# Attention block: row maxima carried to q's extra row by four column transfers a half, in place of a transpose, a copy and one transfer

## Chip, cores and metric

The kernel runs on one core of one Trainium2 chip. The metric is device time in microseconds (us) of one execution; the number compared is the median over runs. All times of the kernel before are from three timed runs and one profiled execution.

## What is computed

The input `x` is (16, 512, 32, 32) float32. Each batch entry is group-normalised over 32 groups, read as 1024 tokens of 512 channels, put through attention with 8 heads of size 64, projected with a bias, and added to `x`. Cut to what matters:

```python
xs  = reshape(group_norm(x), (B, T, C))          # B=16, T=1024, C=512
q   = einsum('btc,hcd->bhtd', xs, Wq)            # the same for k and v
att = softmax(einsum('bhtd,bhsd->bhts', q, k) / 8)
out = einsum('bhts,bhsd->bhtd', att, v)          # heads put side by side
y   = x + reshape(out @ Wproj + bproj, x.shape)
```

## The kernel before

There are 16 batch entries of 8 heads, so 128 heads. A head is worked in one *step* of 16 *slots*. In every slot TensorE (PE) issues two matmuls of scores (`scores`, L708 and L709) three blocks ahead, and three matmuls of probabilities times values (L881 to L883): 128x512 outputs each. ScalarE (ACT) takes the exponential of each block of scores twice (L899, to `prob` and, rounded, to `prob_h`), and GpSimd (POOL, L1294, 13 blocks of 16) or VectorE (DVE, L1043) forms the rounding remainder `prob_l`. A buffer ring of two for `prob` and three for `prob_h` and `prob_l` couples the four engines.

The scores are formed transposed (keys in partitions), so the maximum of a query's row can't be subtracted as a bias. It goes in as a 65th row: `q_lm` has 65 rows, rows 0 to 63 for the low part of q and row 64 (`q_lm[D]`) for the negated row maximum, against a row of ones in `k_h1`. A head's maxima are found during the step before it. Sixteen *row blocks* (`row_scores`, L715, one matmul each into one of two PSUM banks `SM`) have the queries in partitions; DVE reduces each to one column of `smax` (`take_max`, L1106). After row blocks 7 and 15 DVE combines eight columns of `smax` into four columns of `nmax` (`combine`, L1111): the maxima of 512 queries, one 128-query tile a column. That is a *half*. Then, for each half, an entry `mt` of the table follows: PE transposes the four columns into a row bank (`turn_rows`, L700), DVE copies the 4x128 result to `mrow` (`take_rows`, L1117), and the sync engine's queue (SP) issues one transfer of `mrow` to 512 elements of row 64 (`max_row`, L546). PE waits for half 0 at the first score block of the next head, which it issues in slot 13 of the step, and for half 1 at the ninth, which it issues in slot 5 of the next step (`mrow_in`, 16 counts each).

What else PE does stands in a table `WORK` written out by hand, one entry for each kind of step: `plain`, `values`, `norm`, `tokens`, `next`, `proj`, `rows`, `end`. For each slot it lists what is done between scores and values (first tuple) and after the values (second tuple): units of q and k (`qk`, `qn`, 12 matmuls each, L663), of values (`v`, 24 half-width matmuls, L675), transposes of tokens (`xt`, L681), of the projection (`proj`, 12, L693), row blocks (`row`) and `mt`. Between two batch entries the steps are two `values`, `norm`, two `plain`, `tokens`, `next` and `proj`; in the last entry `plain`, `rows` and `end` take the place of those that prepare a next one. `turns` in class `Step` gives the row blocks and the `mt` entries the two `SM` banks in turn and tells PE what to wait for (`turn_free`). Other tables say in which slot DVE takes statistics (`STAT_SLOTS`) and normalises (`NORM_SLOTS`), in which slot the softmax sums travel (`DEN_SLOTS`: `den` from `acc`, L572; `INV_SLOTS`: the reciprocal, L1239; `ROWS_SLOTS`: `inv_dram` L577 and `inv_b` L579; `OUT_SLOTS`: POOL's multiplication, L1321), and `LATE` in which slots ACT copies filler results ahead of the exponentials.

Every engine works through its slots in program order, SP too: an entry in SP's list that waits holds up all behind it. SP also issues the copies of q and k to the other half of the partitions (`twice`, L553 and L555), the inputs and the outputs (L588, L592, L620, L624). A `row` 0 needs the first `twice` of its head, row 4 the second.

Of the kernel before, what the change touches and what calls it, by code (L numbers as in the profile page):

```python
# [5 lines left out]
F32 = mybir.dt.float32  # L6
# [21 lines left out]
        ((("qn", 0, 5),), ()),  # L28
        ((), (("mt", 1, 1), ("qn", 0, 2), ("row", 0, 1))),
        ((), ()),  # L30
        ((), (("qn", 0, 1), ("qn", 1, 1), ("row", 0, 1))),
        ((), (("row", 0, 2),)),
        ((), ()),
        ((("row", 0, 1), ("qn", 1, 1)), (("row", 0, 1),)),
        ((("row", 0, 1),), (("qn", 0, 4), ("row", 0, 2))),
        ((), ()),
        ((("mt", 0, 1), ("row", 0, 1)), ()),
        ((), ()),
        ((("row", 0, 2),), ()),
        ((), (("row", 0, 2),)),  # L40
        ((), (("qn", 1, 10),)),
        ((("row", 0, 2),), ()),
# [3 lines left out]
        ((("v", 0, 13),), ()),  # L46
        ((), (("row", 0, 1), ("mt", 1, 1), ("v", 0, 10))),
        ((("row", 0, 2),), (("v", 1, 2),)),
        ((), (("row", 0, 1),)),
        ((), (("v", 0, 1), ("row", 0, 2))),  # L50
        ((("v", 1, 22), ("row", 0, 1)), (("qn", 0, 2),)),
        ((("row", 0, 1),), (("row", 0, 1),)),
        ((), (("qn", 1, 1), ("qn", 0, 4))),
        ((), ()),
        ((("row", 0, 2), ("qn", 1, 2)), (("mt", 0, 1), ("qn", 0, 5), ("qn", 1, 1))),
        ((), (("row", 0, 2),)),
        ((), ()),
        ((), (("row", 0, 2), ("qn", 0, 1))),
        ((), (("qn", 1, 8),)),
        ((), (("row", 0, 1),)),  # L60
# [5 lines left out]
        ((("mt", 1, 1),), (("row", 0, 2),)),  # L66
        ((), (("row", 0, 1),)),
        ((("row", 0, 1),), (("qn", 0, 1),)),
        ((), (("row", 0, 1),)),
        ((), (("row", 0, 2), ("mean", 0, 1), ("qn", 0, 3))),  # L70
        ((("row", 0, 1),), (("row", 0, 1), ("var", 0, 1))),
        ((), (("mt", 0, 1),)),
        ((), (("qn", 0, 1),)),
        ((), (("row", 0, 1),)),
        ((("qn", 1, 2),), (("qn", 0, 1), ("row", 0, 2))),
        ((), (("qn", 1, 1),)),
        ((("qn", 1, 1),), (("row", 0, 1), ("qn", 1, 2))),
        ((("row", 0, 1),), (("qn", 1, 6),)),
# [15 lines left out]
        ((), ()),
        ((("xt", 4, 4),), ()),
        ((), (("row", 0, 2),)),
# [3 lines left out]
        ((("xt", 5, 4),), ()),  # L100
        ((), (("xt", 6, 4),)),
        ((("mt", 1, 1),), (("qk", 0, 12),)),
        ((), (("xt", 7, 4),)),
        ((), ()),
# [9 lines left out]
        ((), (("row", 0, 2),)),  # L114
        ((), ()),
    ),
    "proj": (
        ((), ()),
        ((("mt", 1, 1),), (("row", 0, 2),)),
        ((), (("row", 0, 2),)),  # L120
        ((), (("row", 0, 2), ("proj", 0, 12))),
        ((), (("row", 0, 2), ("proj", 1, 12))),
        ((), (("row", 0, 1),)),
        ((("mt", 0, 1),), (("proj", 2, 12),)),
        ((), (("proj", 3, 12), ("row", 0, 2))),
        ((), ()),
        ((("proj", 4, 12),), (("row", 0, 1),)),
        ((), (("row", 0, 1), ("proj", 5, 12))),
        ((("row", 0, 1),), (("proj", 6, 12),)),
        ((("row", 0, 1),), (("proj", 7, 12),)),  # L130
        ((), (("qn", 0, 12), ("qn", 1, 10))),
        ((("row", 0, 1), ("qn", 1, 2)), ()),
# [4 lines left out]
        ((), (("mt", 1, 1), ("row", 0, 2))),  # L137
# [7 lines left out]
        ((), (("mt", 0, 1), ("row", 0, 1))),  # L145
# [9 lines left out]
        ((), (("mt", 1, 1),)),  # L155
# [19 lines left out]
STAT_SLOTS = ((1, 4, 4, 5), (3, 3, 5, 7))  # L175

MEAN_SLOTS = (6, 7)

NORM_SLOTS = ((13, 15, 15, 15), (11, 12, 14, 15))

DEN_SLOTS = (9, 1)

INV_SLOTS = (10, 2)
# [3 lines left out]
OUT_SLOTS = (13, 5)  # L187
# [3 lines left out]
EARLY_ROWS, EARLY_OUT = (12, 3), (13, 4)  # L191
# [3 lines left out]
CAST_SLOTS = (0, 1, 2, 3, 4, 6, 7, 9)  # L195
SPLIT_SLOTS = tuple(slot + 1 for slot in CAST_SLOTS)

LATE = {"plain": (0, 1, 2, 3, 4, 6, 7, 8, 9, 13, 14), "tokens": (1, 2, 3, 7, 8, 11, 14), "next": (0, 1, 3, 6, 7, 8, 9, 10, 11, 12, 14, 15), "proj": (4, 5, 7, 8, 12, 14), "values": (2, 3, 5, 6, 8, 9, 10, 13, 14), "norm": (0, 1, 4, 7, 8, 9, 10, 12, 15)}


def step_kind(h, has_next, proj):
    if proj:
        return "proj"
    if h in (1, 2):
# [1186 lines left out]
```

## Time and profile before

| | us |
|---|---|
| median of 3 runs (4452.08 to 4463.26) | 4452.45 |
| profiled execution, its own time | 4452.18 |
| span in the profile, first to last instruction | 4450.4 |
| PE busy with matmuls | 4410.9 (99% of the span) |
| ACT busy | 2952.8 (66%) |
| POOL busy | 2857.7 (64%) |
| DVE busy | 2580.5 (58%) |

How to read it: matmuls are pipelined, so a matmul's duration (396 ns for a 128x512 one) covers more than its turn in the array; the distance from one start to the next tells what it costs. "Busy" says little of whether PE waited a few tenths of a microsecond. The view of waits names what ended each idle stretch, the chain of waits follows the last instruction back to what released it, and the timeline has single instructions in order of time. SPq rows are transfers being issued by the sync engine; the time to landing is counted from the issue.

### The profile page before, as it was taken

To read this page: it belongs to the slowest core of one execution; us is meant where nothing else is said; L and a number is where in the kernel's file an instruction comes from. 1 tells how busy PE (TensorE), PEld (TensorE's weight loads), DVE (VectorE), ACT (ScalarE), POOL (GpSimd) and SP (SyncE) were. 2 spreads that over 40 slices of the span, in tenths; PEclk is the share of its full clock that TensorE was granted. 3 is DMA by queue.
4 is the path that set the end of the run, shared out by engine and by line. 5 is a ranking of instruction groups with operands and counts; after the bars stand their busy time and mean duration, and the time that the engine had idled before them with its cause. 6 is when DMAs were issued, how large, how long until landed. Compare 5 with 4: busy or idle time off the path is not lost.

```text
span 4450.4 us, 61770 instructions
## 1 busy us (share of the span) xinstructions
PE 4410.9 (99%) x20864; PEld 3611.6 (81%) x20864; DVE 2580.5 (58%) x5063; ACT 2952.8 (66%) x5644; POOL 2857.7 (64%) x2227
## 2 busy tenths in 40 slices
PE   8999999999999999999999999999999999999999
PEld 7888888888888888888888888887888888888886
DVE  6655646556465565655656556565664656646454
ACT  5766757667576675756757567575775757757575
POOL 5666666666666566665666656666666666567566
PEclk9999999999999999999999999999999999999999
DMA  3111121211111112111121111211112111121201
GB/s 78 38 53 49 37 61 34 57 45 38 59 37 58 43 35 64 36 60 39 33 70 35 56 39 34 68 38 55 38 33 68 39 57 36 36 66 38 59 25 56
DMA packets 156825, 211.42 MB, mean 48 GB/s; under 512 B 56544, under 2 KB 57568, under 8 KB 156512
## 3 DMA queue, kind: packets, MB, share of 16 engines
q1 hardware_dynamic: 156512, 207.47, 16.5%
q8 instruction: 169, 2.77, 0.3%
q14 instruction: 144, 1.18, 0.1%
HBM read 105.12 MB, written 34.08 MB: 31 GB/s over the span
## 4 chain that ended last, share of the span: by engine, by line
PE 94%; DVE 2%; POOL 1%; ACT 1%; DMA 1%; issue 0%; SPq 0%; POOLq 0%; ACTq 0%; DVEq 0%
PE bank L663 16%; PE bank L715 10%; PE bank L881 10%; PE bank L882 10%; PE bank L883 10%; PE bank L709 10%; PE bank L708 10%; PE bank L675 8%; PE bank L693 8%; PE bank L681 1%; POOL prob_l L1294 1%; PE bank L700 1%; DVE smax L1106 1%; DVE xs L1073 0%; ACT prob L899 0%
## 5 line engine op out<-in xcount | busy, mean ns | idle before, releaser
L1294 POOL TENSOR_TENSOR prob_l<-prob,prob_h 128x512 fp32r<-128x512 f32 x1660 | 2140.5, 1297 | 1437.9 <-ACT prob_h L899 1418.2
L1106 DVE TENSOR_REDUCE smax<-bank 128x1 f32<-128x512 f32 x2048 | 1347.5, 682 | 868.2 <-PE bank L715 864.1
L899 ACT ACTIVATE prob<-bank 128x512 f32<-128x512 f32 x2048 | 1232.2, 602 | 575.3 <-PE bank L709 413.1
L899 ACT ACTIVATE prob_h<-bank 128x512 fp32r<-128x512 f32 x2048 | 1227.2, 599 | 461.9 <-PE bank L883 393.0
L881 PE MATMUL bank<-prob_h,vh 128*128 128x512 f32 x2048 | 822.2, 401 | 7.8 <-ACT acc L1018 4.2
L708 PE MATMUL bank<-q_hh,k_hl 128*128 128x512 f32 x2048 | 813.1, 397 | 0.0
L709 PE MATMUL bank<-q_lm,k_h 65*128 65x512 f32 x2048 | 811.4, 396 | 0.0
L882 PE MATMUL bank<-prob_h,vl 128*128 128x512 f32 x2048 | 806.3, 394 | 0.0
L883 PE MATMUL bank<-prob_l,vh 128*128 128x512 f32 x2048 | 805.8, 393 | 0.0
L715 PE MATMUL bank<-k_hl,q_hh 128*128 128x512 f32 x2048 | 716.4, 402 | 6.2 <-DVE smax L1106 6.0
L881 PEld LDWEIGHTS bank<-prob_h,vh 128*128 128x128 f32 x2048 | 388.8, 190 | 109.8 <-ACT acc L1018 15.4
L715 PEld LDWEIGHTS bank<-k_hl,q_hh 128*128 128x128 f32 x2048 | 379.6, 189 | 109.3 <-DVE smax L1106 26.5
L883 PEld LDWEIGHTS bank<-prob_l,vh 128*128 128x128 f32 x2048 | 384.9, 188 | 88.2
L1043 DVE TENSOR_TENSOR prob_l<-prob,prob_h 128x512 fp32r<-128x512 f32 x388 | 281.8, 726 | 298.1 <-ACT prob_h L899 294.3
L708 PEld LDWEIGHTS bank<-q_hh,k_hl 128*128 128x128 f32 x2048 | 385.4, 188 | 84.4 <-issue 2.9
L882 PEld LDWEIGHTS bank<-prob_h,vl 128*128 128x128 f32 x2048 | 388.1, 189 | 79.0
L709 PEld LDWEIGHTS bank<-q_lm,k_h 65*128 65x128 f32 x2048 | 385.3, 188 | 78.8
L1321 POOL TENSOR_TENSOR o<-acc,inv_b 64x512 f32<-64x512 f32 x256 | 351.9, 1374 | 129.4 <-DMA inv_b<-inv_dram 114.2
L663 PE MATMUL bank<-xh,wqk_h 128*128 128x512 f32 x1024 | 405.7, 396 | 3.7 <-DVE xl L1082 1.8
L663 PE MATMUL bank<-xh,wqk_l 128*128 128x512 f32 x1024 | 402.9, 393 | 0.0
L663 PE MATMUL bank<-xl,wqk_h 128*128 128x512 f32 x1024 | 401.5, 394 | 0.0
L675 PE MATMUL bank<-wv_l,xh 128*128 128x256 f32 x1024 | 291.1, 285 | 0.0
(83 smaller groups left out, 5064.6 us busy)
## 6 DMA issues: line engine op xcount, KB each, us to landing
xs<-in_x SPq DMA_DIRECT2D x252, 256.0 KB, 2.8
q_hh<-q_hh SPq DMA_DIRECT2D x256, 128.0 KB, 2.2
k_hl<-k_h SPq DMA_DIRECT2D x256, 128.0 KB, 2.3
inv_b<-inv_dram SPq DMA_DIRECT2D x256, 128.0 KB, 2.8
out_x<-xs SPq DMA_DIRECT2D x128, 256.0 KB, 2.0
q_lm<-q_lm SPq DMA_DIRECT2D x256, 2.0 KB
den<-acc SPq DMA_DIRECT2D x256, 2.0 KB, 1.7
inv_dram<-inv SPq DMA_DIRECT2D x256, 2.0 KB, 1.4
```

The lines of the kernel that those rows point to most:

```text
L663: last = nc.tensor.matmul(w[:, :], weight[:, c, head, :], moving[:, c, cols], start=u == 0, stop=u == 3 * CH - 1)
L675: last = nc.tensor.matmul(w[:, j * 256:(j + 1) * 256], weight[:, c, t], moving[:, c, vcols], start=cp == 0, stop=cp == 3 * CH - 1)
L693: last = nc.tensor.matmul(w[:, :], left[:, o_set, c, :], right[:, c, :], start=u == 0, stop=u == 3 * CH - 1)
L708: nc.tensor.matmul(s_bank[:, :], k_hl[:, slot, keys], q_hh[:, slot, queries], start=True, stop=False)
L709: nc.tensor.matmul(s_bank[:, :], k_h1[0:D + 1, slot, keys], q_lm[0:D + 1, slot, queries], start=False, stop=True).then_inc(scores_ready, 1)
L715: nc.tensor.matmul(ps[SM + turn][:, :], q_hh[:, slot, t * P:(t + 1) * P], k_hl[:, slot, half * 512:(half + 1) * 512], start=True, stop=Tru ...
L881: nc.tensor.matmul(ps[bank][:, :], v_hi_op, prob_h[:, ring, :], start=t == 0, stop=False)
L882: nc.tensor.matmul(ps[bank][:, :], v_lo_op, prob_h[:, ring, :], start=False, stop=False)
L883: nc.tensor.matmul(ps[bank][:, :], v_hi_op, prob_l[:, ring, :], start=False, stop=t == TT - 1).then_inc(pv_done, 1)
L899: return nc.scalar.activation(out, ps[ST + bank][:, :], ACT.Exp, scale=SCALE)
L1106: nc.vector.tensor_reduce(smax[:, 2 * t + half:2 * t + half + 1], ps[SM + turn][:, :], AX.X, ALU.max).then_inc(rows_used, 1)
L1294: nc.gpsimd.tensor_tensor(prob_l[:, r3, :], prob[:, ring2, :], prob_h[:, r3, :].bitcast(F32), ALU.subtract).then_inc(prob_l_pool, 1)
```

## The change

`mt` entries, `turns`, `turn_rows`, `take_rows`, `mrow` and the semaphores `mt_done` and `mt_used` go. `nmax` is typed float32r, and `combine` writes it as before. SP waits for `nmax_ready` itself and issues four transfers a half, each of one column (128 partitions, one element each) to 128 elements of row 64; `mrow_in` counts 64 for a half. `combine` waits until the half's transfers of the head before have landed. Both halves go at the slot after their last row block. Row block j uses bank j % 2 and waits for row block j - 2. All `WORK` tables, the slot tables and `LATE` are new.

```diff
-        ((), (("mt", 1, 1), ("qn", 0, 2), ("row", 0, 1))),
...
     "tokens": (
+        ((("xt", 0, 4), ("row", 0, 1)), ()),
+        ((), ()),
+        ((("row", 0, 1),), (("row", 0, 1),)),
+        ((), (("xt", 1, 4), ("row", 0, 2), ("xt", 2, 4))),
+        ((), ()),
+        ((), (("xt", 3, 4),)),
+        ((), (("row", 0, 1),)),
+        ((), (("row", 0, 1),)),
         ((("row", 0, 1),), ()),
+        ((("row", 0, 1), ("mean", 1, 1)), ()),
+        ((("row", 0, 2),), (("var", 1, 1),)),
+        ((("row", 0, 1),), (("row", 0, 2),)),
+        ((), ()),
...
     "next": (
...
+        ((("row", 0, 2), ("v", 1, 4), ("v", 2, 7)), (("row", 0, 2), ("v", 2, 16))),
+        ((("row", 0, 1),), (("v", 3, 23), ("row", 0, 2))),
+        ((("v", 3, 1), ("qn", 0, 2)), ()),
+        ((("qn", 0, 7), ("row", 0, 2)), (("qn", 0, 2), ("row", 0, 1))),
+        ((("row", 0, 1),), (("row", 0, 1),)),
...
-DEN_SLOTS = (9, 1)
-INV_SLOTS = (10, 2)
+DEN_SLOTS = (8, 1)
+INV_SLOTS = (11, 2)
 ROWS_SLOTS = (12, 4)
-OUT_SLOTS = (13, 5)
+OUT_SLOTS = (14, 5)
...
-        nmax = sb("nmax", [P, TT])
-        mrow = q_lm[96:100, 0, 0:2 * P].rearrange("p (a q) -> p a q", a=2)
+        nmax = sb("nmax", [P, TT], F32R)
...
-            def max_row(half, slot):
-                sp.dma_start(q_lm[D:D + 1, slot, half * 512:(half + 1) * 512].bitcast(F32),
-                             mrow[:, half, :].bitcast(F32)).then_inc(mrow_in[half], 16)
+            def max_row(half, slot, count):
+                sp.wait_ge(nmax_ready, count)
+                for t in range(4 * half, 4 * half + 4):
+                    sp.dma_start(q_lm[D:D + 1, slot, t * P:(t + 1) * P].bitcast(F32),
+                                 nmax[:, t:t + 1].bitcast(F32)).then_inc(mrow_in[half], 16)
...
-                    for a in s.issued(i - 1, "mt"):
-                        mt_taken(sp, s, a)
-                        max_row(a, (s.k + 1 - a) % 2)
+                    for hj in s.rows_in(i - 1) if i else ():
+                        if hj in (7, 15):
+                            max_row(hj // 8, (s.k + 1) % 2, s.heads(2, 1, hj // 8 + 1))
...
-            def turn_rows(a, turn):
-                nc.tensor.transpose(ps[SM + turn][0:4, 0:P], nmax[:, a * 4:(a + 1) * 4], ident[:, :]).then_inc(mt_done, 1)
...
-                            _, _, bank, user = s.turn("row", j)
-                            turn_free(s, user)
-                            row_scores((s.k + 1) % 2, j, bank)
+                            pe.wait_ge(rows_used, s.heads(BLOCKS, 1, j - 1))
+                            row_scores((s.k + 1) % 2, j, j % 2)
...
-                                pe.wait_ge(mrow_in[0], s.heads(16, 1, 16))
+                                pe.wait_ge(mrow_in[0], s.heads(64, 1, 64))
...
-                                pe.wait_ge(mrow_in[1], s.heads(16, 0, 16))
+                                pe.wait_ge(mrow_in[1], s.heads(64, 0, 64))
...
-            def combine(half, used):
+            def combine(half, used, read):
                 dve.wait_ge(rows_used, used)
+                if read:
+                    dve.wait_ge(mrow_in[half], read)
...
-            def take_rows(half, turn, count):
-                dve.wait_ge(mt_done, count)
-                nc.vector.tensor_copy(mrow[:, half, :], ps[SM + turn][0:4, 0:P]).then_inc(mt_used, 1)
```

Where the entries stand in the tables of before and after (slot, and a or b for the first or the second tuple; the units of filler in the slots are those that the whole diff lists):

| step | before: row 7, mt half 0, row 15, mt half 1 (next step) | after: row 4, row 7, row 15 | after: PE's work from the slot after row 7 to slot 12, in matmuls of 128x512 (two of half width count as one) |
|---|---|---|---|
| plain | 7b, 9a, 14a, 1b | 5a, 6b, 14a | slots 7 to 12: 40 |
| values | 6a, 9b, 14b, 1b | 3a, 5b, 13b | 6 to 12: 59 |
| norm | 6b, 8b, 14a, 2a | 5b, 7b, 13a | 8 to 12: 38 |
| tokens | 8b, 10b, 14b, 1a | 3b, 8a, 13a | 9 to 12: 27 |
| next | 9b, 10b, 14b, 2a | 8b, 9b, 14b | 10 to 12: 31 |
| proj | 4b, 6a, 14a, 1a | 4b, 5b, 14b | 6 to 12: 114 |

Slots with two or more row blocks: 42 in the eight steps of a batch entry before, 36 after.

## Rows read from the trace of the kernel before

**Rows 1.** The page: engines over the span; PE and its clock in 40 slices.
```profile
PE 4410.9 (99%) x20864; PEld 3611.6 (81%) x20864; DVE 2580.5 (58%) x5063; ACT 2952.8 (66%) x5644; POOL 2857.7 (64%) x2227
...
PEclk9999999999999999999999999999999999999999
```

**Rows 2.** The page: the chain that ended last, by engine.
```profile
PE 94%; DVE 2%; POOL 1%; ACT 1%; DMA 1%; issue 0%; SPq 0%; POOLq 0%; ACTq 0%; DVEq 0%
```

**Rows 3.** The view of waits, whole span: us in total, times, longest us.
```profile
PEld bank L715 <- DVE smax L1106: 26.5, 83, 1.4
...
PEld bank L881 <- ACT acc L1018: 15.4, 35, 1.1
...
PE bank L715 <- DVE smax L1106: 6.0, 22, 1.0
...
PEld bank L715 <- DVE q_lm L1117: 3.8, 16, 0.5
```

**Rows 4.** Groups by line: shapes, count | busy us, mean ns | idle before, releaser.
```profile
L1117 DVE CAST q_lm<-bank 4x128 fp32r<-4x128 f32 x256 | 72.6, 284 | 85.1 <-PE bank L700 80.7
...
L700 PE MATMUL bank<-ident,nmax 128*4 128x128 f32 x256 | 69.8, 273 | 0.0
```

**Rows 5.** The timeline of PE around one transpose: start, duration, line.
```profile
1006.96 0.40 PE L883 MATMUL bank<-prob_l,vh 128*128 128x512 f32 x1
1007.20 0.27 PE L700 MATMUL bank<-ident,nmax 128*4 128x128 f32 x1
1007.22 0.48 PE L663 MATMUL bank<-xl,wqk_h 128*128 128x512 f32 x1
1007.54 0.39 PE L663 MATMUL bank<-xh,wqk_h 128*128 128x512 f32 x1
```

**Rows 6.** The chain of waits, whole span, longest pieces: start us, us, what.
```profile
851.32 2.98 PE bank L663 x13
...
1126.60 2.98 PE bank L663 x13
```

**Rows 7.** The chain of waits around another transpose: start us, us, what.
```profile
1119.08 0.11 PE bank L700
1119.18 0.23 PE bank L708
```

**Rows 8.** The view of one line: SP's issues of the maxima (L546).
```profile
L546 SPq DMA_DIRECT2D q_lm<-q_lm x256: 599/653/724, 43.8 to 4401.3; - x128
```

**Rows 9.** The timeline of SP: start and duration of issues.
```profile
11.19 1.05 SPq L535 DMA_DIRECT2D o<-in_L_conv_Wk  x1
...
1000.99 0.49 SPq L553 DMA_DIRECT2D q_hh<-q_hh  x1
1001.53 0.59 SPq L555 DMA_DIRECT2D k_hl<-k_h  x1
```

**Rows 10.** The view of SP's own waits: us in total, times, longest.
```profile
SPq L546 <- DVE q_lm L1117: 968.7, 241, 12.1
```

**Rows 11.** The timeline, step `next` of one batch entry: slots 10 and 13.
```profile
1116.44 0.40 PE L708 MATMUL bank<-q_hh,k_hl 128*128 128x512 f32 x1
...
1117.73 0.16 DVE L1111 TENSOR_REDUCE nmax<-smax 128x4 f32<-128x8 f32 x1
...
1125.28 0.40 PE L708 MATMUL bank<-q_hh,k_hl 128*128 128x512 f32 x1
```

**Rows 12.** The page: DMA issues, count, KB each, median us to landing.
```profile
q_hh<-q_hh SPq DMA_DIRECT2D x256, 128.0 KB, 2.2
...
den<-acc SPq DMA_DIRECT2D x256, 2.0 KB, 1.7
```

**Rows 13.** The page: all DMA packets, and SP's queue with its share.
```profile
DMA packets 156825, 211.42 MB, mean 48 GB/s; under 512 B 56544, under 2 KB 57568, under 8 KB 156512
...
q1 hardware_dynamic: 156512, 207.47, 16.5%
```

**Rows 14.** The timeline of POOL: six remainders back to back.
```profile
1018.99 7.64 POOL L1294 TENSOR_TENSOR prob_l<-prob,prob_h 128x512 fp32r<-128x512 f32 x6
```

More of the change, by code:

```diff
@@ L136 @@
         ((), ()),
-        ((), (("mt", 1, 1), ("row", 0, 2))),
+        ((), (("row", 0, 2),)),
         ((), (("row", 0, 1),)),
@@ L144 @@
         ((), (("row", 0, 1),)),
-        ((), (("mt", 0, 1), ("row", 0, 1))),
+        ((), (("row", 0, 1),)),
         ((), (("row", 0, 1),)),
@@ L154 @@
         ((), ()),
-        ((), (("mt", 1, 1),)),
+        ((), ()),
         ((), ()),
@@ L173 @@
 TAKE_QN = 13
-STAT_SLOTS = ((1, 4, 4, 5), (3, 3, 5, 7))
-MEAN_SLOTS = (6, 7)
-NORM_SLOTS = ((13, 15, 15, 15), (11, 12, 14, 15))
-DEN_SLOTS = (9, 1)
-INV_SLOTS = (10, 2)
+STAT_SLOTS = ((1, 2, 2, 5), (5, 6, 8, 8))
+MEAN_SLOTS = (6, 8)
+NORM_SLOTS = ((12, 12, 14, 14), (12, 12, 14, 14))
+DEN_SLOTS = (8, 1)
+INV_SLOTS = (11, 2)
 ROWS_SLOTS = (12, 4)
-OUT_SLOTS = (13, 5)
+OUT_SLOTS = (14, 5)
 END_DEN, END_INV, END_ROWS, END_OUT = (8, 0), (10, 3), (10, 4), (12, 5)
 END_BIAS = (9, 11)
-EARLY_ROWS, EARLY_OUT = (12, 3), (13, 4)
+EARLY_ROWS, EARLY_OUT = (12, 2), (14, 5)
 PROJ_SLOTS = tuple(slot for slot, sides in enumerate(WORK["proj"]) for kind, a, n in sides[0] + sides[1] if kind == "proj" and n == 12)
-CAST_SLOTS = (0, 1, 2, 3, 4, 6, 7, 9)
+CAST_SLOTS = (0, 1, 2, 5, 6, 7, 8, 9)
 SPLIT_SLOTS = tuple(slot + 1 for slot in CAST_SLOTS)
-LATE = {"plain": (0, 1, 2, 3, 4, 6, 7, 8, 9, 13, 14), "tokens": (1, 2, 3, 7, 8, 11, 14), "next": (0, 1, 3, 6, 7, 8, 9, 10, 11, 12, 14, 15), "proj": (4, 5, 7, 8, 12, 14), "values": (2, 3, 5, 6, 8, 9, 10, 13, 14), "norm": (0, 1, 4, 7, 8, 9, 10, 12, 15)}
+LATE = {"plain": (4, 9, 13, 14, 15), "tokens": (0, 1, 4, 5, 6, 9, 10, 12, 14, 15), "next": (0, 1, 2, 3, 5, 6, 7, 8, 9, 10, 11, 13, 14, 15), "proj": (2, 6, 7, 9, 13), "values": (0, 1, 3, 4, 6, 8, 9, 10, 11, 12, 14, 15), "norm": (3, 4, 5, 6, 7, 8, 10, 11, 13, 15)}
 def step_kind(h, has_next, proj):
@@ L217, in fillers @@
             for kind, a, n in items:
-                if kind in ("row", "mt"):
+                if kind == "row":
                     slot += [(side, kind, a, 0, 1)] * n
@@ L256, in __init__ @@
                     for side, kind, a, lo, hi in slot:
-                        if kind in ("row", "mt"):
+                        if kind == "row":
                             continue
@@ L293, in __init__ @@
         self.out_slots = EARLY_OUT if self.proj else END_OUT if end else OUT_SLOTS
-        self.turns, user = [], [None, None]
-        for kind, a in [(e[1], e[2]) for slot in self.slots or [] for e in slot if e[1] in ("row", "mt")]:
-            n = sum(e[0] == "row" for e in self.turns)
-            bank = len(self.turns) % 2
-            self.turns.append((kind, n if kind == "row" else a, bank, user[bank]))
-            user[bank] = (kind, n if kind == "row" else a)
     def at(self, per_batch, const):
@@ L318, in bank @@
         return bank, n
-    def turn(self, kind, a):
-        return next(e for e in self.turns if e[:2] == (kind, a))
     def issued(self, slot, kind):
@@ L477, in entry_taken @@
             eng.wait_ge(taken[bank], before + 1)
-        def mt_taken(eng, s, a):
-            eng.wait_ge(mt_used, s.heads(2, 0 if a else 1, 2 if a else 1))
         def start_taken(eng, kind, a):
@@ L768, in _ @@
                     v_units += hi - lo
-                if j == 9:
-                    pe.wait_ge(nmax_ready, 1)
-                    pe.wait_ge(rows_used, 9)
-                    turn_rows(0, 0)
                 if j == 13:
-                    scores(0, 0, 0, lambda: pe.wait_ge(mrow_in[0], 16))
+                    scores(0, 0, 0, lambda: pe.wait_ge(mrow_in[0], 64))
                     scores(0, 1, 1, nothing)
@@ L778, in _ @@
             pe.wait_ge(v_cols, 2)
-            def turn_free(s, user):
-                if user is None:
-                    pe.wait_ge(rows_used, s.heads(BLOCKS, 1))
-                    pe.wait_ge(mt_used, s.heads(2, 0, 1))
-                elif user[0] == "row":
-                    pe.wait_ge(rows_used, s.heads(BLOCKS, 1, user[1] + 1))
-                else:
-                    mt_taken(pe, s, user[1])
             def work_free(s, kind, a):
@@ L822, in other_work @@
                     if at != side:
-                        continue
-                    if kind == "mt":
-                        _, _, bank, user = s.turn("mt", a)
-                        turn_free(s, user)
-                        pe.wait_ge(nmax_ready, s.heads(2, 0 if a else 1, 2 if a else 1))
-                        turn_rows(a, bank)
                         continue
@@ L1159, in _ @@
             for j in range(BLOCKS):
-                take_max(j, j + 1, (j + (j > 9)) % 2)
+                take_max(j, j + 1, j % 2)
                 if j == 1:
@@ L1192, in step @@
                         if kind == "row":
-                            take_max(hj, s.heads(BLOCKS, 1, hj + 1), s.turn("row", hj)[2])
+                            take_max(hj, s.heads(BLOCKS, 1, hj + 1), hj % 2)
                             if hj in (7, 15):
-                                combine(hj // 8, s.heads(BLOCKS, 1, hj + 1))
+                                combine(hj // 8, s.heads(BLOCKS, 1, hj + 1), s.heads(64, 0, 64))
                             hj += 1
-                        if kind == "mt":
-                            take_rows(a, s.turn("mt", a)[2], s.heads(2, 0 if a else 1, 2 if a else 1))
                     if j not in pool_blocks_of(s, ahead) and not (end and ahead):
```

119 lines of the change are left out of this document (49 added, 70 removed), and 15 rows, old and new, of the table WORK.

## The prediction

> **What bounds the kernel now.** First the page. PE is busy for 4410.9 of 4450.4 us, at the full granted clock, and the next engine, ACT, for 66% [rows 1]. Busy time alone would not settle it, since matmul ends are modelled, so the second view is the chain that ended last: 94% of it is PE [rows 2]. The third is the view of waits [rows 3]: what PE waits for in 128 heads is tens of us, with row blocks waiting for DVE's maxima first (26.5 us at the weight load, 6.0 us at the matmul) and the accumulator's copy by ACT next (15.4 us). So the kernel is a stream of matmuls with few holes; an instruction taken out of it is worth its place in it, and nothing else is worth much unless it opens or shuts a hole. 0.3%, or 13.4 us, is about what a measurement of this kernel can tell from no change.
>
> **PE: 256 transposes go.** The page of groups gives them 273 ns each, 69.8 us together [rows 4]. That is not what they cost. In the timeline the matmul ahead of one starts at 1006.96 and the second one behind it at 1007.54 [rows 5]; the two 128x512 matmuls in that stretch would take 2 x 0.232 = 0.464 us at their usual pitch (thirteen in a row take 2.98 us, 0.229 each [rows 6]; mixed with semaphore waits 0.23 to 0.24; I take 0.232; 1007.22 is the late start of the first one behind, and its 0.48 us hold the transpose's share). 0.58 - 0.464 = 0.116 us. The chain has the same transpose form with 0.11 us against 0.23 for a matmul [rows 7]. 256 x 0.116 = **29.7 us**. Bounds: 256 x 0.10 = 26 us and 256 x 0.12 = 31 us, the resolution of those rows. All of it lies on the path, because the matmul behind is ready in nearly every case.
>
> **DVE: 256 copies go**, 284 ns each, 72.6 us, and with them 80.7 us in which DVE stood waiting for the transpose [rows 4]. DVE is busy 58% of the time [rows 1], so the copies themselves are worth nothing on the path; what covers them is PE's stream, and without that cover they would be in it. Indirectly they can be worth something: the next `take_max` stands behind the copy, and row blocks wait for `take_max`. Bounds: nothing, and all of 26.5 + 6.0 + 3.8 us, the waits of row blocks for maxima and for the copy [rows 3]. Slots with two or more row blocks, where such waits arise, fall from 42 to 36 of a batch entry. I take 2 us and keep the rest for the range. The wait that `combine` gains is for transfers of a head ago, about 30 us old: nothing, and nobody is held behind it. Typing `nmax` float32r changes one 160 ns instruction's output and nothing in time.
>
> **SP: 256 issues go, 1024 come.** One issue of the old form takes 0.65 us [rows 8], so a half held SP for 0.65 us and now holds it for four issues. No row has a transfer with 128 runs of 4 bytes. The neighbours: 64 runs in 0.49 and 0.59 us, 1024 runs of the weights in 1.05 us [rows 9]. I take 0.65 us, the row with the same destination; bounds 0.45 and 1.05 us. A half then holds SP 2.6 us (1.8 to 4.2). SP waited 968.7 us at just this place [rows 10], so 256 x 3 x 0.65 = 499 us more of issuing fits in; the question is only what gets late.
>
> *Half 0 in time?* In step `next`, the maxima are in `nmax` at 1117.73 + 0.16 = 1117.89, 1.45 us after slot 10 began (1116.44), and PE begins slot 13 at 1125.28 [rows 11]. In the new table slots 10 to 12 hold 31 matmuls, 31 x 0.232 = 7.3 us, so the window is 7.3 - 1.45 = 5.8 us. The same sum gives for `tokens` 27 x 0.232 - 0.75 = 5.5 us (row 7 stands ahead of three value matmuls there, which takes 0.7 us off the 1.45), `norm` 7.4, `plain` 7.8, `values` 12 and `proj` 25 us. Needed: a wait's end and three issue pitches of 0.69 us, then the last transfer's landing. The nearest landings are 1.7 us (sums, 2 KB) and 2.2 us (q, 128 KB) [rows 12]; with the longer, 3 x 0.69 + 2.2 = 4.3 us. It fits with 1.2 us to spare, and I count **0 us**. With 1.05 us an issue it is 3.3 + 2.2 = 5.5 us, still just in time. Half 1 has from slot 14 or 15 to slot 5 of the next step, over 6 us everywhere but for the very last head, and is no closer.
>
> *What is queued behind four issues?* In steps `values` and `proj` the second `twice` of the next head stands behind half 1 in SP's list. From `proj` to `values`: row 4 comes after slots 15 and 0 to 2, 34.6 matmuls and two scores, 8.5 us. Maxima at 1.45, four issues to 4.05, the first of `twice`'s two issues 0.55 us, and the second landing 2.2 us after its start: 1.45 + 2.6 + 0.55 + 2.2 = 6.8 us, 1.7 us to spare, room for 4.3 us of issues. From `values` to `values` it is slots 14, 15 and 0 to 2, 39.6 matmuls and two scores, 9.6 us: room for 5.4 us. The transfers of the softmax sums (slots 8, 12) wait at most 2.6 us, and the new tables give them one slot more from `den` to the multiplication. 0 us.
>
> *The transfers themselves.* 156,512 packets took 16.5% of 16 engines' span [rows 13]: 0.165 x 4450 x 16 / 156,512 = 75 ns each, most of them 2 KB long. The change adds 131,072 packets of 4 bytes and a few per transfer for counting. At 75 ns each, eight elements on each of 16 engines take 0.6 us, less than an issue's pitch, so they keep up; the share rises to at most 32%. Bounds for what that does to others' transfers: nothing, and 0.3 us on each of the 256 `inv_b`, hidden behind POOL's later slot. I take 1 us in all, for the start of the kernel, where the first scores follow the first maxima closely.
>
> **Sum.** 4452.2 (the profiled execution's own time) - 29.7 - 2 + 1 = 4421.5, and the median of the runs is 0.3 us above that execution: **4422 us**, 0.7% faster.
>
> The Trainium skill, "DMA: Bandwidth & Descriptors", section "Rules for kernel authors", speaks against the change: many small transfers should be coalesced into one, and under 64 KB one pays mostly overhead. With the about 2 us of fixed cost that the page fits for one transfer, paid one after another, a half would need 8 us, and the gain would be gone. The trace shows overlap instead: the second of a pair is issued 0.54 us after the first [rows 9], while the first takes 2.2 us to land [rows 12].
>
> **Rivals.**
> *A. Column transfers run one after another (slower).* Place: SP's queue between `nmax_ready` and slot 13, and the `twice` behind it. Price: 1.7 us a column, the landing of the sums [rows 12], if 128 short writes into one partition don't overlap. 4 x 1.7 = 6.8 us a half: late by 1.0 us in `next`, 1.3 in `tokens`, and behind it `twice` by 6.8 - 4.3 = 2.5 us from `proj` to `values` and 1.4 us from `values` to `values`. 6.2 us x 15 batch entries = 93 us, less 31: **4514 us**. It cancels the gain from about 1.44 us a column (2.1 us an entry) and is slower by 0.3% from 1.50. For it: no row shows this form; against it: the pairs that overlap. 0.07.
> *B. The new order waits more (no change).* The gain is in the stream, but every table is new. POOL makes six remainders in 7.64 us, 1.27 each [rows 14], against 5 x 0.232 = 1.16 us of PE in a slot without filler, and ACT's and DVE's places are moved too. The rows of PE's waits shown add up to 51.7 us [rows 3]; half as much again, 0.2 us a head, takes 26 us back: **4447 us**. For it: PE has no slack of its own, and it now carries 0.23 us less a head to cover the others with. Against it: POOL, ACT and DVE have a third of their time free. 0.15.
> *C. DVE's relief counts (faster still).* Half of the row blocks' waits (36.3 us) go: 18 us on top of the transposes: **4405 us**. For it: those waits are the largest; against it: they arise as well where two row blocks stand together. 0.13.
> That the change doesn't do what it says has no room: the transposes can't stay in the stream once they are not issued.
>
> **How the numbers follow.** The forecast has 0.65, and its own range is 4412 to 4436: the transposes' bounds and a few us of waits either way. Range for 8 in 10: 4407 to 4443, into C and up to the near side of B; A and B's far side are left out. Faster by over 0.3% means under 4439: the forecast nearly whole (0.63), C (0.13) and a little of B (0.03) make 0.79. Same: the rest of the forecast, most of B and the narrow part of A, 0.14. Slower: 0.07.
>
> **What would show it.** No L700 and no L1117 in the groups; L546 with 1024 issues near 0.65 us; packets near 300,000; starts of matmuls still 0.232 us apart; distance between the same points of two batch entries down from 275.3 us (851.32 to 1126.60 [rows 6]) by 16 x 0.116 = 1.9 us. Wrong if the score matmul at slot 13 of `next` or `tokens`, or row 4 after `proj`, starts late behind a transfer; if L546 issues take over 1.05 us; or if PE's waits for DVE, ACT or POOL grow by over 15 us.

## The result and the profile after

The changed kernel takes 4469.12 us (median of 6 runs, 4466.59 to 4471.58) against 4452.77 us for the one before beside it (6 runs): a ratio of 1.0034 with a 95% interval from 1.0021 to 1.0047. It was to be 0.7% faster and is 0.3% slower. The profiled execution took 4467.35 us, its span is 4465.4 us.

The page of the changed kernel, for [rows 1, 12, 13]: engines, packets, SP's queue and the landings (count, KB each, median us).

```profile
PE 4400.4 (99%) x20608; PEld 3608.9 (81%) x20608; DVE 2568.6 (58%) x4807; ACT 2968.5 (66%) x5644; POOL 2840.0 (64%) x2227
...
DMA packets 302235, 211.46 MB, mean 47 GB/s; under 512 B 202976, under 2 KB 202976, under 8 KB 301920
...
q1 hardware_dynamic: 301920, 207.53, 17.9%
...
q_lm<-nmax SPq DMA_DIRECT2D x1024, 0.5 KB, 2.0
```

The view of the line that now issues the maxima (shortest, median and longest ns), for [rows 8].

```profile
L531 SPq DMA_DIRECT2D q_lm<-nmax x1024: 468/601/1824, 42.7 to 4412.7; - x171
```

The 256 transposes are gone, TensorE has 256 instructions and 10.5 us of busy time less, its clock is as before (9 in every slice of the page), the 1024 issues take 0.60 us each, and 145,400 more packets raise the share of the DMA engines by 1.4 points only. All of that is at or under its estimate (the share was bounded at 32%). What went wrong is in the view of waits (us in total, times, longest), for [rows 3]:

```profile
DVE inv L1189 <- DMA den<-acc: 85.2, 59, 5.1
...
PE bank L696 <- DVE smax L1062: 34.8, 54, 2.1
PEld bank L696 <- DVE smax L1062: 34.2, 78, 2.1
PEld bank L696 <- issue: 32.9, 30, 2.5
...
DVE bn L1005 <- DMA xs<-in_x: 25.6, 18, 2.5
```

Row blocks (L696, L715 before) wait 34.8 us for maxima at the matmul, where they waited 6.0 us [rows 3], and 32.9 us more of their weight loads, in 30 places, have no releaser that the profile shows (in e1 below that row is gone; I take them for the same wait, which the profile does not say). On the line above stands a wait that [rows 3] did not even list, since it is not PE's: DVE's reciprocal for the transfer of the softmax sums. In the kernel before the same view has it as

```profile
DVE inv L1239 <- DMA den<-acc: 52.4, 32, 5.8
...
DVE bn L1049 <- DMA xs<-in_x: 4.1, 4, 2.4
```

so 27 waits of it are new. DVE's wait for the next input (`xs`) is new too, 25.6 us for 4.1; it comes back under e11.

*Where in the batch entry.* This is the distance from the first score matmul of one step to that of the next, read from PE's timeline and summed over the 15 full batch entries, in us (values and plain are two steps each). The last two columns are the experiments e1 and e10 below:

| step | before | after | e1 | e10 |
|---|---|---|---|---|
| values | 1013.2 | 1007.3 | 1007.4 | 1007.4 |
| norm | 428.7 | 426.2 | 426.2 | 426.2 |
| plain | 840.7 | 834.6 | 834.7 | 834.6 |
| tokens | 394.2 | 399.8 | 388.3 | 400.5 |
| next | 699.7 | 704.1 | 703.9 | 704.1 |
| proj | 762.2 | 780.0 | 753.2 | 758.6 |
| sum | 4138.7 | 4152.0 | 4113.7 | 4131.4 |
| first step (once) | 29.1 | 31.6 | 31.7 | 31.7 |

In values, norm and plain the gain is there: 14.5 us for the 150 transposes of these 75 steps, 0.097 us each. `tokens`, `next` and `proj` lost 5.6, 4.4 and 17.8 us and the first step 2.6 us; the steps behind the last full entry gained 1.7 us. Together +14.2 of the span's +15.0 us.

*What happens in `proj`.* The timeline of the changed kernel in slots 0 to 4 of one `proj` (start us, us, engine, what; in brackets the idle time before it and what ended it):

```profile
1141.35 0.58 ACT L974 COPY acc<-bank 128x512 f32<-128x512 f32 x1
1141.37 2.44 SPq L531 DMA_DIRECT2D q_lm<-nmax  x4
...
1143.86 0.60 SPq L538 DMA_DIRECT2D q_hh<-q_hh  x1
...
1145.20 0.54 SPq L573 DMA_DIRECT2D xs<-in_x  x1
...
1145.79 0.55 SPq L557 DMA_DIRECT2D den<-acc  x1
...
1146.26 0.62 PE L696 MATMUL bank<-k_hl,q_hh 128*128 128x512 f32 x2
...
1148.10 0.24 DVE L1189 RECIPROCAL inv<-den 32x16 f32<-32x16 f32 x1 [2.31 <-DMA den<-acc]
1148.27 2.56 DVE L1062 TENSOR_REDUCE smax<-bank 128x1 f32<-128x512 f32 x4
...
1149.03 1.00 PE L696 MATMUL bank<-k_hl,q_hh 128*128 128x512 f32 x2 [1.00 <-DVE smax L1062]
```

Read it from the end. PE stands 1.00 us at 1149.03 for `take_max`. DVE took the two row blocks that PE had made by 1146.9 only from 1148.27 on, since the reciprocal of the head's second tile stands ahead of them in DVE's list and waited 2.31 us for its sums. They were in `acc` at 1141.93, but SP issued their transfer at 1145.79: four columns of half 1 (2.44 us), then three transfers that waited behind them. The same place in the kernel before:

```profile
1132.38 0.58 ACT L1018 COPY acc<-bank 128x512 f32<-128x512 f32 x1
1132.99 0.55 SPq L572 DMA_DIRECT2D den<-acc  x1
...
1134.90 0.67 SPq L546 DMA_DIRECT2D q_lm<-q_lm  x1
1135.51 1.29 DVE L1106 TENSOR_REDUCE smax<-bank 128x1 f32<-128x512 f32 x2 [0.64 <-PE bank L715]
...
1136.72 0.23 DVE L1239 RECIPROCAL inv<-den 32x16 f32<-32x16 f32 x1
```

There the sums went 0.61 us after their copy began, the maxima behind them, and the reciprocal waited for nothing. In the changed kernel the order is the other way round and the sums went 4.44 us after it. By the gaps in PE's list this takes 1.85 us at slot 4 of a `proj` and 1.2 us at slot 3 of a `tokens`, where the same chain runs:

```profile
1068.22 2.44 SPq L531 DMA_DIRECT2D q_lm<-nmax  x4
...
1070.70 0.60 SPq L557 DMA_DIRECT2D den<-acc  x1
...
1072.54 0.24 DVE L1189 RECIPROCAL inv<-den 32x16 f32<-32x16 f32 x1 [1.53 <-DMA den<-acc]
1072.92 2.63 DVE L1062 TENSOR_REDUCE smax<-bank 128x1 f32<-128x512 f32 x4
1073.66 0.50 PE L696 MATMUL bank<-k_hl,q_hh 128*128 128x512 f32 x1 [0.68 <-DVE smax L1062]
```

In full it is 1.49 + 0.36 us in `proj` and 0.75 + 0.45 us in `tokens`, 15 x 3.05 = 45.8 us of gaps, against the 29.7 us that the transposes were to give.

### The profile page after: what moved, and what is told of

Its sections match the earlier page's. It is cut to its first block and busy times, and to the rows that moved or that the text cites. A ratio compares the mean times of both kernels' runs of the same rounds, so it can differ in the third digit from the quotient of the medians.

```text
span 4465.4 us, 61626 instructions
## 1 busy us (share of the span) xinstructions
PE 4400.4 (99%) x20608; PEld 3608.9 (81%) x20608; DVE 2568.6 (58%) x4807; ACT 2968.5 (66%) x5644; POOL 2840.0 (64%) x2227
## 2 busy tenths in 40 slices
DMA packets 302235, 211.46 MB, mean 47 GB/s; under 512 B 202976, under 2 KB 202976, under 8 KB 301920
## 3 DMA queue, kind: packets, MB, share of 16 engines
q1 hardware_dynamic: 301920, 207.53, 17.9%
## 5 line engine op out<-in xcount | busy, mean ns | idle before, releaser
L696 PE MATMUL bank<-k_hl,q_hh 128*128 128x512 f32 x2048 | 731.3, 400 | 35.5 <-DVE smax L1062 34.8
L999 DVE TENSOR_TENSOR prob_l<-prob,prob_h 128x512 fp32r<-128x512 f32 x388 | 339.4, 875 | 429.1 <-ACT prob_h L855 428.9
L696 PEld LDWEIGHTS bank<-k_hl,q_hh 128*128 128x128 f32 x2048 | 383.1, 189 | 152.4 <-DVE smax L1062 34.2
L1271 POOL TENSOR_TENSOR o<-acc,inv_b 64x512 f32<-64x512 f32 x256 | 332.1, 1297 | 26.3 <-POOL prob_l L1244 7.5
L660 PE MATMUL bank<-wv_h,xl 128*128 128x256 f32 x1024 | 287.8, 282 | 0.0
```

The source lines that it names most:

```text
L696: nc.tensor.matmul(ps[SM + turn][:, :], q_hh[:, slot, t * P:(t + 1) * P], k_hl[:, slot, half * 512:(half + 1) * 512], start=True, stop=Tru ...
L999: nc.vector.tensor_tensor(prob_l[:, r3, :], prob[:, ring2, :], prob_h[:, r3, :].bitcast(F32), ALU.subtract).then_inc(prob_l_ready, 1)
L1271: nc.gpsimd.tensor_tensor(o[r, h // 2, tc * 512:(tc + 1) * 512], acc[r, tc, :], inv_b[r, :], ALU.mult).then_inc(o_ready, 1)
```

## The experiments

The theory: half 1's four issues stand ahead of the sums in SP's queue; the reciprocal then holds DVE's maxima, and these hold PE. The rivals: the traffic of 131,072 packets of 4 bytes slows the other transfers (order would not matter then), and the new tables themselves wait more, with no part of the transfers in it.

**e1: the same transfers, in the other order.** Half 1's four transfers go right behind the sums of slot 1; everything else is the changed kernel.

```diff
                 if i == s.den_slots[1] and not first:
                     den_to_square(s, -1, 1)
+                    max_row(1, s.k % 2, s.heads(2, 0, 2))
                 for hj in s.rows_in(i - 1) if i else ():
-                    if hj in (7, 15):
-                        max_row(hj // 8, (s.k + 1) % 2, s.heads(2, 1, hj // 8 + 1))
+                    if hj == 7:
+                        max_row(0, (s.k + 1) % 2, s.heads(2, 1, 1))
```

> The changed kernel, but half 1's four column transfers are issued in slot 1 of the next step, behind the transfer of the softmax sums, and no longer ahead of it. Theory 'order': in the changed kernel four issues (2.44 us) stand ahead of the sums' transfer in SP's list; the sums land late, DVE's reciprocal waits for them in slot 2 and the row maxima stand behind it, so PE loses 1.5 + 0.36 us in slot 4 of proj and 0.75 + 0.45 us in slot 3 of tokens, 15 times each, 46 us in all. Then this kernel takes 4422 to 4436 us and those gaps are gone. Theory 'traffic' (1024 transfers of 128 short runs slow the others) and theory 'tables' (the new order of work is worse by itself): both 4465 to 4472 us, as the changed kernel.

Measured: 4428.06 us against 4457.52 us, ratio 0.9939 [0.9922, 0.9956], the fastest version here; it beats both kernels. The timeline of its `proj`:

```profile
1129.60 0.58 ACT L975 COPY acc<-bank 128x512 f32<-128x512 f32 x1
...
1130.88 0.55 SPq L557 DMA_DIRECT2D den<-acc  x1
...
1131.47 2.52 SPq L531 DMA_DIRECT2D q_lm<-nmax  x4
...
1133.96 0.23 DVE L1190 RECIPROCAL inv<-den 32x16 f32<-32x16 f32 x1
```

and its waits:

```profile
PEld bank L697 <- DVE smax L1063: 29.6, 75, 2.1
DVE bn L1006 <- DMA xs<-in_x: 26.2, 18, 2.4
...
PE bank L697 <- DVE smax L1063: 8.0, 20, 1.7
...
DVE inv L1190 <- DMA den<-acc: 6.5, 3, 5.8
```

The sums go 1.28 us after their copy began, the reciprocal's wait falls from 85.2 to 6.5 us and that of the row blocks from 34.8 to 8.0 us. By the table `proj` gets 26.8 us back and `tokens` 11.5; all other steps are as in the changed kernel. That is 38.3 of the 45.8 us of gaps: in `tokens` the gaps of slot 3 go, but slots 8 and 9, where DVE waits for `xs`, take 6.7 us more. The packets are the same 302,235, so traffic is not the cause.

**e2: one transfer a half.** With the queries of a row block taken with a stride of four, query 4p + t goes to block t, and then the four columns of a half are one transfer of 128 runs of 16 bytes. The place in SP's list is the changed kernel's.

```diff
-                for t in range(4 * half, 4 * half + 4):
-                    sp.dma_start(q_lm[D:D + 1, slot, t * P:(t + 1) * P].bitcast(F32),
-                                 nmax[:, t:t + 1].bitcast(F32)).then_inc(mrow_in[half], 16)
+                sp.dma_start(q_lm[D:D + 1, slot, half * 512:(half + 1) * 512].bitcast(F32),
+                             nmax[:, 4 * half:4 * half + 4].bitcast(F32)).then_inc(mrow_in[half], 16)
...
+                queries = q_hh[:, slot, (t // 4) * 512:(t // 4 + 1) * 512].rearrange("p (q t) -> p t q", t=4)[:, t % 4, :]
-                nc.tensor.matmul(ps[SM + turn][:, :], q_hh[:, slot, t * P:(t + 1) * P],
+                nc.tensor.matmul(ps[SM + turn][:, :], queries,
```

> The changed kernel with its tables, but one transfer a half: a row block takes every fourth query of its half as its weights, so that the four columns of nmax lie in the order of row 64 and go there in one transfer of 128 runs of 16 bytes. Theory 'order': the hold on SP falls from 2.44 to about 0.6 us, the sums land 1.8 us earlier, 4422 to 4436 us. Theory 'traffic': packets fall from 302,000 to about 200,000, which gives back part, 4435 to 4460 us. Theory 'tables': 4465 us or more. If weights read with a stride of four load slower than the 190 ns that a matmul of 232 ns hides, up to 2048 x 0.04 = 80 us on top, seen in the weight loads of the row blocks.

Measured: 4447.76 us, 0.9978 [0.9968, 0.9987]: 9.8 us faster than the one before, 19.7 us slower than e1. The groups by line of e2 (mean ns behind the busy us), and the same one of e1:

```profile
L696 PEld LDWEIGHTS bank<-k_hl,q_hh 128*128 128x128 f32 x2048 | 596.9, 310 | 74.8 <-DVE smax L1062 9.5 <-issue 1.8
```

```profile
L697 PEld LDWEIGHTS bank<-k_hl,q_hh 128*128 128x128 f32 x2048 | 382.0, 189 | 114.7 <-DVE smax L1063 29.6
```

A strided weight load takes 310 ns, not 189. Most of that is still covered, though it is longer than a matmul's pitch of 0.232 us: from one row block to another right behind it the median distance is 0.238 us for 0.233 in e1, and over 0.3 us in 67 of 572 places for 17. A step (16 row blocks) of values or plain takes some 0.2 us more than in e1 (33.81 for 33.58, 27.99 for 27.82), `next` and `proj` 0.3 us more, `norm` and `tokens` no more. Over the 15 entries e2 comes out 17.4 us above e1. That the stride is the cause is argued from the loads, not shown by a run of its own. As a test of order against traffic this run is muddied by that cost, and only e1 carries that verdict.

**e3: the column transfers in the old tables.** The tables and slots of the kernel before, without the transposes, the copies and the waits of a row block for them; the four columns go at the place where the old transfer went.

```diff
-                        mt_taken(sp, s, a)
-                        max_row(a, (s.k + 1 - a) % 2)
+                        max_row(a, (s.k + 1 - a) % 2, s.heads(2, 0 if a else 1, 2 if a else 1))
...
-                        turn_rows(a, bank)
```

> The kernel before with all its tables and slots; transposes and copies are left out and the four column transfers a half are issued where the one was. Half 1's stand in slot 2 or 3 of the next step, behind the sums. Theory 'order': nothing is delayed that DVE waits for at its maxima, the transposes' 29.7 us are gained: 4420 to 4432 us. Theory 'traffic': the gain of the transposes is eaten here too, 4450 us or more. Theory 'tables': 4420 to 4432 us, as 'order' (the first run tells these two apart).

Measured: 4446.49 us, 0.9977 [0.9967, 0.9986]: 11.0 us faster, less than half of what the expectation gave. In steps without new gaps two transposes are worth 0.25 us (33.77 to 33.52 in values, 27.97 to 27.72 in the second plain step), 0.125 us each. The rest was lost again. In `tokens` PE's transposes of the tokens wait for DVE's norm, 1.07 us in each entry, 16 us; other gaps of that step shrank, and it came out 6.4 us longer than before. The timeline of e3 there, then that of the kernel before:

```profile
1080.55 1.28 POOL L1254 TENSOR_TENSOR prob_l<-prob,prob_h 128x512 fp32r<-128x512 f32 x1
...
1080.62 1.49 DVE L1039 TENSOR_SCALAR xs<-xs,gmean,rstd 128x512 f32<-128x512 f32 x1 [2.04 <-POOL rstd L1231]
...
1082.26 0.63 PE L674 MATMUL bank<-ident,xs 128*128 128x128 f32 x4 [0.82 <-DVE xs L1039]
```

```profile
1080.88 0.55 DVE L1073 TENSOR_SCALAR xs<-xs,gmean,rstd 128x512 f32<-128x512 f32 x1 [1.72 <-POOL rstd L1271]
...
1081.13 1.44 POOL L1294 TENSOR_TENSOR prob_l<-prob,prob_h 128x512 fp32r<-128x512 f32 x1 [0.29 <-ACT prob_h L899]
```

The norm is the same instruction. Where POOL's remainder started 0.07 us ahead of it, it takes 1.49 us and ends 0.28 us behind POOL; where it started 0.25 us ahead of POOL, it takes 0.55. The first plain step lost 5.4 us in the same way: the last of its norms takes 1.66 us for 0.54, DVE comes late to the maxima, and row blocks in slot 4 stand 8.3 us in all. So a table of its own is part of the change's gain: e1 has one and is 18 us faster than e3.

**e4 and e9: three more issues in the kernel before, ahead of or behind the maxima.** They write to a row that nothing reads. The lines are e4's, with a wait for the earlier spare transfers left out; e9 has the loop below the last line.

```diff
             def max_row(half, slot):
+                for t in range(3):
+                    sp.dma_start(q_lm[D + 1:D + 2, half, t * P:(t + 1) * P].bitcast(F32),
+                                 ident[:, t:t + 1]).then_inc(spare_in[half], 16)
                 sp.dma_start(q_lm[D:D + 1, slot, half * 512:(half + 1) * 512].bitcast(F32),
```

> The kernel before as it is, with three column transfers (of a constant, to an unused row) added ahead of each of its 256 transfers of maxima: the cost of 768 issues and 98,304 short runs alone, in an order in which the sums' transfer stands ahead of half 1. Theory 'order': 4450 to 4458 us, no change. Theory 'traffic': the 45 us that the changed kernel lost against its forecast appear here, 4490 us or more. Theory 'tables': no change.

> The kernel before with three column transfers (of a constant, to an unused row) added behind each of its 256 transfers of maxima; in the fourth experiment they stood ahead and it took 4555 us. If that loss came from the maxima themselves landing 1.8 us later in an order that has no room for it, it is gone here but for what stands behind in SP's list: 4450 to 4475 us. If 98,304 short runs cost by their traffic, it stays: 4530 us or more.

Measured: e4 4554.95 us, 1.0223 [1.0208, 1.0239]; e9 4522.41 us, 1.0154 [1.0137, 1.0171]. Under 'order' e4 was expected at 4458 us at most and e9 at 4475, so both missed, by 97 and 47 us; e4 lies where 'traffic' had put it, e9 between its two ranges. They missed by the same step as the prediction: they asked for the transfer's own lateness and not for the queue behind. The waits of e4, then of e9, then of the kernel before:

```profile
POOL o L1328 <- DMA inv_b<-inv_dram: 325.6, 152, 5.0
...
PE bank L715 <- DMA q_lm<-q_lm: 52.3, 45, 1.8
```

```profile
POOL o L1327 <- DMA inv_b<-inv_dram: 373.5, 171, 4.4
...
PEld bank L887 <- POOL prob_l L1300: 42.3, 64, 2.7
```

```profile
POOL o L1321 <- DMA inv_b<-inv_dram: 114.2, 96, 3.0
```

In e4 the maxima land late for the score matmul, the cause that e9 was made to take away. In both, the transfers of the reciprocals stand behind 1.8 us more of issues and POOL waits for them some 210 and 260 us longer; in e9 PE then waits for POOL's remainders. That e9, with as many packets, is 32.5 us faster than e4, and that values and the second plain step are unchanged to 0.01 us in both (33.77 and 27.97), speaks for order and against traffic. The lost time stands in `norm`, the first plain step and `tokens` (14.8, 13.5 and 37.1 us in e9). The changed kernel does not suffer this: with its slot more from `den` to the multiplication POOL hardly waits.

```profile
POOL o L1271 <- DMA inv_b<-inv_dram: 1.1, 1, 1.1
```

**e5: two columns ahead of the sums, two behind.**

```diff
                     den_to_square(s, -1, 1)
+                    max_row(1, s.k % 2, s.heads(2, 0, 2), range(2, 4))
...
+                    if hj == 15:
+                        max_row(1, (s.k + 1) % 2, s.heads(2, 1, 2), range(2))
```

> The changed kernel with half 1's four column transfers split: two stay ahead of the sums' transfer, two go behind it. Theory 'order': the lateness grows with the number of issues ahead, 0.61 us each. Two less bring the sums 1.2 us forward, so that PE's 1.49 us gap in slot 4 of proj falls to about 0.3 us and the 0.75 and 0.45 us in slot 3 of tokens to near nothing: between the first experiment's 4428 and the changed kernel's 4469, near the former, 4428 to 4438 us. If only whether the sums' transfer is first or second mattered (the transfers lock each other out), about 4450 us or more.

Measured: 4446.15 us, 0.9979 [0.9970, 0.9988]: between four ahead (ratio 1.0034) and none ahead (0.9939), so the cost grows with what stands ahead, but 8 us above the expected. Half the issues left about half the loss, in `proj` 8.1 of 26.8 us (761.3 us in the table's terms) and in `tokens` 8.3 of 11.5 (396.6 us). Slot 4 of `proj` is 0.56 us longer than in e1, where 0.3 was expected, and the gap at slot 3 of `tokens` is gone, as expected. What the expectation had not seen is that slots 8 and 9 of `tokens` take 7.3 us more over the 15 entries than in e1, with DVE's wait for `xs` at 34.7 us in place of 26.2. The reciprocal itself still waits 31 times, 31.2 us.

**e7 and e10: SP's order left alone, the reciprocal moved down DVE's list,** in `proj` only: from slot 2 to slot 3 (e7) or 4 (e10), with what uses it moved on.

```diff
-EARLY_ROWS, EARLY_OUT = (12, 2), (14, 5)
+EARLY_ROWS, EARLY_OUT = (12, 4), (14, 6)       # e10; e7: (12, 3), (14, 5)
...
-        self.inv_slots = END_INV if end else INV_SLOTS
+        self.inv_slots = (11, 4) if self.proj else END_INV if end else INV_SLOTS   # e7: (11, 3)
```

> The changed kernel, SP's order untouched, but in proj steps DVE takes the reciprocal of the late sums in slot 3 in place of 2, behind two more row maxima (and SP sends it on in slot 3 too). Theory 'order': what costs time is not the late transfer itself but DVE's wait for it ahead of the maxima; with the wait behind them the gap of 1.5 + 0.36 us in slot 4 of proj goes or shrinks to under 0.5 us, 15 times, and the one in tokens stays: 4438 to 4450 us. If the late transfer hurt by itself (POOL's multiplication or the traffic): 4465 us or more.

> The changed kernel, SP's order of issues of the maxima and the sums untouched, but in proj steps DVE takes the late reciprocal in slot 4, really behind the maxima of row blocks 2 and 3 (in the run before it stood in slot 3, still ahead of them, so that nothing could change), SP sends it on in slot 4 and POOL multiplies in slot 6. Theory 'order, through DVE's list': the gap of 1.5 us ahead of row block 4 in proj goes, with the 0.36 us behind it, 15 times, and the gap in tokens stays: 4438 to 4450 us. If the row block waits for something else that the four issues delay (the second twice): 4465 us or more.

Measured: e7 4469.86 us, 1.0034 [1.0022, 1.0046], no different from the changed kernel; e10 4446.17 us, 0.9986 [0.9977, 0.9995], as expected. In e7 the reciprocal is one slot later but still ahead of the maxima of row blocks 2 and 3 in DVE's list, so the edit does not touch the chain; its expectation rested on a wrong reading of that list. In e10 it is behind them:

```profile
1141.85 1.29 DVE L1062 TENSOR_REDUCE smax<-bank 128x1 f32<-128x512 f32 x2 [0.91 <-PE bank L696]
...
1143.47 0.24 DVE L1189 RECIPROCAL inv<-den 32x16 f32<-32x16 f32 x1 [0.33 <-DMA den<-acc]
```

The reciprocal still waits for its sums, PE no longer does: `proj` falls from 780.0 to 758.6 us, and `tokens`, whose reciprocal was not moved, keeps its loss (400.5 us). This is the link between reciprocal and maxima, shown with SP's order of issues of sums and maxima as it was. The 5.4 us that `proj` still has over e1 are a new gap in slot 8, where PE waits for ACT's copy of the accumulator. That this copy is late because of POOL's later multiplication is likely but not shown.

**e11: e1 with the loads of the next tokens ahead of the reciprocals' transfers,** for the 26.2 us that e1's DVE waits for `xs` (4.1 us before the change).

```diff
-                    if i == s.rows_slots[1] and not first:
-                        inv_to_rows(s, -1, 1)
...
+                    if i == s.rows_slots[1] and not first:
+                        inv_to_rows(s, -1, 1)
```

> The first experiment's kernel (4428 us), and in SP's list the loads of the next input go ahead of the reciprocal's two transfers in the same slot, the second of which waits for the first to land. In that kernel DVE waits 26 us for these loads with the statistics, in steps tokens, and the maxima of row blocks stand behind; PE's gaps in slots 8 and 9 of tokens sum to 10 us. Theory 'order': those 26 us and gaps mostly go, 4416 to 4424 us. If they come from the load's own 3 us of landing: no change, 4425 to 4430 us.

Measured: 4442.65 us, 0.9978 [0.9968, 0.9987], slower than e1 and not what was expected. The wait for `xs` is 27.1 us as in e1, but it is another load that is waited for. SP's timeline of e11 in slots 2 to 6 of one `tokens`:

```profile
787.82 3.55 SPq L608 DMA_DIRECT2D xs<-in_x  x3
791.42 0.43 SPq L562 DMA_DIRECT2D inv_dram<-inv  x1
794.22 0.50 SPq L564 DMA_DIRECT2D inv_b<-inv_dram  x1
794.76 0.59 SPq L608 DMA_DIRECT2D xs<-in_x  x1
```

In e1 the second and third load stand behind the reciprocal's two transfers, and DVE waits 1.46 us (median of 15) for the second. In e11 these two go at 6.4 and 7.3 us into the step instead of 7.7 and 8.4, and that wait is gone. But the reciprocal's transfers now stand behind them, and the fourth load stands behind the second of these, which waits for the first to land: it goes at 11.05 us instead of 10.10, DVE waits 1.44 us for it, and the maxima stand behind that wait: slot 9 takes 14.2 us more over the 15 entries than in e1, slot 8 3.1 us less. With what POOL waits for its reciprocals, `tokens` takes 401.2 us for 388.3:

```profile
POOL o L1272 <- DMA inv_b<-inv_dram: 23.6, 13, 2.9
```

## Why the prediction was wrong

*The step that failed* is in the part on what is queued behind four issues: "The transfers of the softmax sums (slots 8, 12) wait at most 2.6 us, and the new tables give them one slot more from `den` to the multiplication. 0 us." Two things are wrong in it. It looked at half 0's place alone. The second transfer of the sums, in slot 1, stands behind half 1's four issues and, in `proj`, behind the `twice` and the load that these push back, 4.44 us after the copy began instead of 0.61. And it followed the sums to their last user, POOL's multiplication, and not to the first, DVE's reciprocal, with what stands behind that in DVE's list: the maxima, for which PE's next row blocks wait. The prediction put this at nothing. Measured: 45.8 us of gaps in the changed kernel, and 41 us between it and e1 by their medians (by the two ratios, 1.0034 - 0.9939 = 0.0095 of 4453 us, it is 42). The transposes' 29.7 us less these 45.8 us are +16 us, and +16.4 us was measured, but that the sum comes out so closely is luck: the order gives 38.3 us back in `proj` and `tokens`, the 0.097 us of a transpose in the clean steps make 25 us of 256 and not 29.7, and the new tables lose and gain in other places.

*The transposes* (29.7 us, 0.116 each) held: 0.097 each in the steps of the changed kernel without new gaps, 0.125 in e3; the 273 ns of the groups [rows 4] would have been more than twice too much. e1 comes out at 4428.06 us, 29.5 us below the kernel before beside it, where the forecast was 30 us below; its interval is 20 to 35 us, and by the spans of the two profiled executions it is 25.7 us. Part of the match is luck: against the kernel before, e1 loses in the first step (+2.6 us, I had 1 us) and in `next` (+4.2 us, of it 0.37 us an entry for a gap that stood in `proj` before) and gains more than the transposes in `tokens` (-5.9 us) and `proj` (-9.0 us).

*DVE's relief* (2 us) is not to be seen in the changed kernel, where row blocks wait 69.0 us for maxima in place of 32.5; in e1 it is 37.6 us, no relief by that row. The fall from 42 to 36 that it was argued from counts tuples, not slots; by slots it is 46 to 41, and in `proj` it rises from 5 to 6.

*SP's issues:* 0.60 us for my 0.65, and half 0 is in time in `next` and `tokens`: no wait of the score matmul for a column of maxima appears. (31 x 0.232 is 7.2 us and not 7.3, which changes nothing.) `twice` behind four issues cost PE nothing by itself that I can find. SP waits 1002 us for the maxima now, 968.7 before [rows 10]: a queue with a thousand us of idle time is still late at one place for 4 us.

```profile
SPq L531 <- DVE nmax L1069: 1002.1, 256, 16.7
```

*The transfers:* the share rose to 17.9%, for a bound of 32%: 1.4 points for 145,400 packets, an estimate of 7 ns each and not the 75 ns of the mean packet. The rule of the Trainium skill that the prediction weighed ("DMA: Bandwidth & Descriptors", "Rules for kernel authors": coalesce) speaks against the change, and the change lost, but not for that reason. Four transfers were issued in 2.44 us and each landed 2.0 us after its issue, so they overlap, and e1 keeps all of them and gains. What the runs show against many transfers is only that each one takes its issue, 0.60 us, in SP's list, where the rest stands behind it.

*The rivals.* A (column transfers one after another) is not what happened. B (the new order waits more) was the nearest in its views, PE's waits growing; its place, though, was put in the tables and the engines' pace, not in SP's queue, and its price was 26 us where the gaps were 45.8. C was not reached, by e1 (4428 us) neither. The sign that I had named, PE's waits for DVE growing by over 15 us, did come: +36.5 us.

## What to carry to other kernels

When issues are added to an in-order queue, take each transfer behind them and follow it to its first user, then down that user's list to whoever waits on the bounding engine: here SP, DMA, DVE's reciprocal, DVE's maxima, PE, with each queue far from full. Put the transfer with the least slack first and the bulk behind it: with the same four transfers the kernel is 0.3% slower than before when they go ahead of one small transfer, and 0.6% faster when they go behind it. Moving an issue forward moves others back, as e11 shows. A busy share, of an engine or of a queue, answers none of this.

## What was not expected of the hardware

- Weights read with a stride of four elements of fp32 load in 310 ns for 189 (e2). Though that is longer than a matmul's pitch of 0.232 us, the median distance between two such matmuls is 0.238 us.
- DVE's scale and shift of 128x512 fp32 in SBUF takes 0.54 us with no POOL instruction beside it (60 of 124 in the changed kernel) and 1.49 us when POOL's remainder started first (e3). The Trainium skill, "SBUF — State Buffer", section "Who interferes with whom", says that only the port pair that VectorE and GpSimd share contends, as an exclusive lock. The two timelines agree: DVE ended 0.28 us behind POOL in the one and was not held in the other. So a shift of 0.3 us between the two costs PE 1 us.
- 1024 transfers of 128 runs of 4 bytes took 0.60 us each to issue and 2.0 us to land (e2's single ones of 128 runs of 16 bytes 0.51 and 1.9 us), and together 1.4 points of the DMA engines' time.
